# A layer norm's normalising pass and its bf16 copy, moved from VectorE to ScalarE

## The chip, the cores and the metric

The kernel runs on all eight NeuronCores of one Trainium2 chip, each with its own slice of the batch. Nothing is exchanged between the cores. The metric is the device time of the slowest core in microseconds.

## What is computed

Two "hybrid" layers, four stages in all, on x of shape (8, 2048, 1024) in f32. Each core has one batch element: 2048 tokens of 1024 features.

```python
x = x + attn_a(layernorm(x))   # stage 0: second layer norm inside with gamma, beta;
                               # qkv, causal softmax attention, 16 heads of 64
x = x + ffn(layernorm(x))      # stage 1
x = x + attn_b(layernorm(x))   # stage 2: no mask, projection with bias
x = x + ffn(layernorm(x))      # stage 3
# layernorm(x) = (x - mean) / sqrt(var + 1e-5)
# ffn: silu(bl(x, w_gate)) * bl(x, w_up), then bl(., w_down); inner size 4096
# bl: rows of x rounded to 8 bits by their own maximum, weights rounded to -1, 0, 1
```

## The kernel before

X stays in SBUF for the whole program as 16 token tiles of 128 partitions x 1024 f32. A list of operations is written in program order; each names what it reads and writes, and from that the program sets semaphore waits, also between two instructions of the same engine (TensorE excepted). Each engine then runs its own part of the list strictly in order. X counts as one resource, whichever tile is meant.

At first the three FFN weights are quantised and written to DRAM (until about 545 us). Then come the four stages. Each of them begins its work on a token tile with `ln_tile`:

1. VectorE sums the row (L390), ScalarE squares it with an accumulated sum (L393, into the scratch tile `stg`).
2. `stats`: five small VectorE instructions (L398 to L410), Ln and Exp on ScalarE (L413, L416) for 1/sqrt, and on VectorE mean times that (L419).
3. The normalising pass L425 from X into `xnf`, f32, 128x1024.
4. In mode "ln2" (stage 0) the sum (L429), the squares (L432) and `stats` once more, then L437 and the two passes for gamma and beta (L441, L444). In mode "quant" (stages 1 and 3) the row maximum (L448), three small ones, and ScalarE's scaling to int16 (L463) and copy to bf16 `stg` (L466). In the modes "ln2" and "plain" (stages 0 and 2) the bf16 copy is L469 on VectorE.
5. TensorE transposes `stg` in eight matmuls against the identity (L474) into PSUM, VectorE copies the result to `actT` (L482).

In the attention stages each tile's `ln_tile` is followed by `vunit`: 16 matmuls of the V product (L517) and its copy to `Vaug` on VectorE (L526). WV, the weights of it, are loaded once at the stage's beginning. `xnf` and `stg` are single buffers. Behind the 16 tiles come the projections to Q and K (L555), pass A for the row maxima (L590 to L647) and pass B with the exponentials on ScalarE (L676, L686, L701).

The FFN stages work in eight batches of two tiles: `ln_tile` for both, the gate and up products (L863, L875) with Silu on ScalarE (L885) and the product on VectorE (L892), and behind them the down projection of the batch before (L958 to L981), which ends with X += ... (L995). So the next batch's `ln_tile` reads an X that has just been written. The gate and up weights are fetched in two halves from the POOL queue, the down weights `Wdsl` in double-buffered strips from the SP queue.

Of the kernel before, what the change touches and what calls it, by code (L numbers as in the profile page):

```python
# [19 lines left out]
AF = mybir.ActivationFunctionType  # L20
ALU = mybir.AluOpType
AXX = mybir.AxisListType.X

B, T, D, H = 8, 2048, 1024, 16
# [87 lines left out]
def build_nc():  # L112
# [41 lines left out]
    def sb(name, shape, dtype, at=None):  # L154
        o = cur[0] if at is None else at
        t = nc.alloc_sbuf_tensor_at(name, shape, dtype, offset=o)
        offs[name] = o
        nbytes = int(np.prod(shape[1:])) * mybir.dt.size(dtype)
        cur[0] = o + (nbytes + 31) // 32 * 32
        return t  # L160

    X = sb("X", [128, NTT * D], F32)
# [4 lines left out]
    xnf = sb("xnf", [128, D], F32)  # L167
    stg = sb("stg", [128, D], BF16)
    stat = sb("stat", [128, 48], F32)
# [53 lines left out]
    E = S.emit  # L223
# [50 lines left out]
    def quant_matrix(midx, w_src, rows, cols, tag, dstT):  # L274
# [110 lines left out]
        reads=("swscr",), writes=("invsw_bc",))  # L385
    S.barrier()

    def ln_tile(mode, tt):
            xt = X[:, tt * D:(tt + 1) * D]
            E("dve", lambda e, x=xt: e.tensor_reduce(stat[:, 0:1], x, AXX,  # L390
                                                     ALU.add),
              reads=("X",), writes=("st0",))
            E("act", lambda e, x=xt: e.activation(stg[:, :], x, AF.Square,  # L393
                                                  accum_out=stat[:, 1:2]),
              reads=("X",), writes=("st1", "stg"))

            def stats(c_sum, c_sq, c_r, c_mr):
                E("dve", lambda e, cs=c_sum: e.tensor_scalar(  # L398
                    stat[:, 24:25], stat[:, cs:cs + 1], 1.0 / D, None,
                    ALU.mult), reads=("st%d" % c_sum,), writes=("stm",))  # L400
                E("dve", lambda e: e.tensor_tensor(
                    stat[:, 25:26], stat[:, 24:25], stat[:, 24:25], ALU.mult),
                  reads=("stm",), writes=("stm2",))
                E("dve", lambda e, cq=c_sq: e.tensor_scalar(
                    stat[:, 26:27], stat[:, cq:cq + 1], 1.0 / D, None,
                    ALU.mult), reads=("st%d" % c_sq,), writes=("stq",))
                E("dve", lambda e: e.tensor_tensor(
                    stat[:, 26:27], stat[:, 26:27], stat[:, 25:26],
                    ALU.subtract), reads=("stm2", "stq"), writes=("stq",))
                E("dve", lambda e: e.tensor_scalar(  # L410
                    stat[:, 26:27], stat[:, 26:27], LN_EPS, None, ALU.add),
                  reads=("stq",), writes=("stq",))
                E("act", lambda e: e.activation(stat[:, 27:28], stat[:, 26:27],  # L413
                                                AF.Ln),
                  reads=("stq",), writes=("stln",))
                E("act", lambda e, cr=c_r: e.activation(  # L416
                    stat[:, cr:cr + 1], stat[:, 27:28], AF.Exp, scale=-0.5),
                  reads=("stln",), writes=("st%d" % c_r,))
                E("dve", lambda e, cr=c_r, cm=c_mr: e.tensor_tensor(  # L419
                    stat[:, cm:cm + 1], stat[:, 24:25], stat[:, cr:cr + 1],  # L420
                    ALU.mult), reads=("stm", "st%d" % c_r),
                  writes=("st%d" % c_mr,))

            stats(0, 1, 2, 3)
            E("dve", lambda e, x=xt: e.tensor_scalar(  # L425
                xnf[:, :], x, stat[:, 2:3], stat[:, 3:4], ALU.mult,
                ALU.subtract), reads=("X", "st2", "st3"), writes=("xnf",))
            if mode == "ln2":
                E("dve", lambda e: e.tensor_reduce(stat[:, 4:5], xnf[:, :],  # L429
                                                   AXX, ALU.add),  # L430
                  reads=("xnf",), writes=("st4",))
                E("act", lambda e: e.activation(stg[:, :], xnf[:, :],  # L432
                                                AF.Square,
                                                accum_out=stat[:, 5:6]),
                  reads=("xnf",), writes=("st5", "stg"))
                stats(4, 5, 6, 7)
                E("dve", lambda e: e.tensor_scalar(  # L437
                    xnf[:, :], xnf[:, :], stat[:, 6:7], stat[:, 7:8], ALU.mult,
                    ALU.subtract), reads=("xnf", "st6", "st7"),
                  writes=("xnf",))  # L440
                E("dve", lambda e: e.tensor_tensor(  # L441
                    xnf[:, :], xnf[:, :], gamma_bc[:, :], ALU.mult),
                  reads=("xnf", "gamma_bc"), writes=("xnf",))
                E("dve", lambda e: e.tensor_tensor(  # L444
                    xnf[:, :], xnf[:, :], beta_bc[:, :], ALU.add),
                  reads=("xnf", "beta_bc"), writes=("xnf",))
            if mode == "quant":
                E("dve", lambda e: e.tensor_reduce(  # L448
                    stat[:, 8:9], xnf[:, :], AXX, ALU.max,
                    apply_absolute_value=True), reads=("xnf",),  # L450
                  writes=("st8",))
                E("dve", lambda e: e.tensor_scalar(
                    stat[:, 8:9], stat[:, 8:9], 1e-5, None, ALU.max),
                  reads=("st8",), writes=("st8",))
                E("dve", lambda e: e.reciprocal(stat[:, 9:10], stat[:, 8:9]),
                  reads=("st8",), writes=("st9",))
                E("dve", lambda e: e.tensor_scalar(
                    stat[:, 9:10], stat[:, 9:10], 127.0, None, ALU.mult),
                  reads=("st9",), writes=("st9",))
                E("dve", lambda e, tt=tt: e.tensor_scalar(  # L460
                    stat[:, 32 + tt:33 + tt], stat[:, 8:9], 1.0 / 127.0, None,
                    ALU.mult), reads=("st8",), writes=("rsx%d" % tt,))
                E("act", lambda e: e.activation(  # L463
                    qsc[:, :], xnf[:, :], AF.Copy, scale=stat[:, 9:10]),
                  reads=("xnf", "st9"), writes=("qsc",))
                E("act", lambda e: e.activation(stg[:, :], qsc[:, :], AF.Copy),  # L466
                  reads=("qsc",), writes=("stg",))
            else:
                E("dve", lambda e: e.tensor_copy(stg[:, :], xnf[:, :]),  # L469
                  reads=("xnf",), writes=("stg",))  # L470
            par = tt % 2
            pk = ("A0", "A1") if par == 0 else ("A2", "A3")
            for ic in range(NIC):
                E("pe", lambda e, ic=ic, p=par: e.matmul(  # L474
                    PA[:, p * 1024 + ic * 128:p * 1024 + (ic + 1) * 128],
                    stg[:, ic * 128:(ic + 1) * 128], ident[:, :],
                    start=True, stop=True),
                  reads=("stg", "ident"), writes=pk,
                  inc="pe" if ic == NIC - 1 else None)
            dstv = actT[:, :].rearrange("p (c t) -> p c t", c=NIC)[  # L480
                :, :, tt * 128:(tt + 1) * 128]
            E("dve", lambda e, p=par, dv=dstv: e.tensor_copy(  # L482
                dv, PA[:, p * 1024:(p + 1) * 1024].rearrange(
                    "p (c t) -> p c t", c=NIC)),
              reads=pk, writes=("actT%d" % tt,))

    def ln_stage(mode, hook=None):
        for tt in range(NTT):
            ln_tile(mode, tt)
            if hook is not None:  # L490
                hook(tt)
# [335 lines left out]
    def ffn():  # L827
# [174 lines left out]
        for bat in range(NTT // 2):  # L1002
            ln_tile("quant", 2 * bat)
            ln_tile("quant", 2 * bat + 1)
            gateup(bat, tail_quant_units(bat - 1) if bat > 0 else ())
            if bat > 0:
                tail_down(bat - 1)
# [107 lines left out]
```

How the kernel before makes its waits and increments, by code:

```python
        def replay(engine, eng):  # L1068
            for (e, fn, waits, inc, n) in S.ops:
                if e != engine:
                    continue
                best = {}
                for (sname, v) in waits:
                    if v > best.get(sname, -1):
                        best[sname] = v
                for sname, v in sorted(best.items()):
                    if v > 0 and last_wait.get((engine, sname), -1) < v:
                        eng.wait_ge(sems[sname], v)
                        last_wait[(engine, sname)] = v
                if fn is None:
                    continue
                inst = fn(eng)
                if inc is not None:
                    inst.then_inc(sems[inc], n)
```

## Time and profile before

| | before |
|---|---|
| median of three runs | 8256.87 us (8251.48, 8256.87, 8267.48) |
| profiled execution | 8252.33 us, span of its slowest core 8250.8 us |
| spans of the eight cores | 8218.4 to 8250.8 us |
| busy share of TensorE / VectorE / ScalarE | 61% / 35% / 20% |
| mean granted clock of TensorE | 0.65 |

The span runs from the first to the last instruction of the slowest core; the profiled execution's time is 1.5 us longer, for what lies around it. Shares are averages over stages with different limits. The kernel has no engine near full, so the question at each place is which engine's work the others wait for.

### The profile page before, as it was taken

How to read it: one execution, taken by the hardware profiler on the slowest of the kernel's cores; microseconds unless marked ns; L12 is line 12 of the kernel's file. 1: busy time of each engine (PE TensorE's matmuls, PEld its weight loads, DVE VectorE, ACT ScalarE, POOL GpSimd, SP SyncE). 2: the span in 40 equal slices, each digit the busy share in tenths (PEclk: the TensorE clock that was granted, in tenths of full speed). 3: DMA queues.
4: the chain of work that ended last, by engine and by line, in shares of the span. 5: the costliest groups of instructions: out<-in, count | busy, mean ns of one | idle time of the engine just before them, and what ended most of it. 6: DMA issues, size and time to landing. Idle time of an engine off the chain costs nothing.

```text
span 8250.8 us, 61625 instructions; the slowest of 8 cores (8218.4 to 8250.8 us)
## 1 busy us (share of the span) xinstructions
PE 4997.0 (61%) x15758; PEld 1588.6 (19%) x15942; DVE 2920.6 (35%) x5756; ACT 1677.2 (20%) x2784; POOL 423.2 (5%) x637
## 2 busy tenths in 40 slices
PE   0223266666666576666645777787777757666675
PEld 0111011111111222222211111111111123222221
DVE  2445233333333333323334244324333434323331
ACT  0321022222222211111001322332333221111110
POOL 0100000000000101000000000000000001000000
PEclk9856555555555688777776555555555568777876
DMA  8850300000000355444310000000000005444553
GB/s 226 287 185 0 45 1 3 3 3 3 3 3 1 105 153 171 138 142 131 119 32 6 2 2 3 3 1 3 3 3 1 1 13 173 145 144 133 153 154 120
DMA packets 260557, 580.78 MB, mean 70 GB/s; under 512 B 78396, under 2 KB 95548, under 8 KB 259772
## 3 DMA queue, kind: packets, MB, share of 16 engines
q0 software_dynamic: 101968, 400.97, 16.3%
q1 hardware_dynamic: 137388, 150.69, 6.8%
q10 hardware_dynamic: 20864, 25.17, 0.9%
q8 instruction: 145, 2.38, 0.1%
q14 instruction: 192, 1.57, 0.1%
HBM read 543.07 MB, written 48.50 MB: 72 GB/s over the span
## 4 chain that ended last, share of the span: by engine, by line
PE 40%; DVE 19%; DMA 18%; ACT 9%; issue 8%; another core or an unknown queue 2%; POOL 1%; DVEq 1%; ACTq 0%; SPq 0%; POOLq 0%; PEldq 0%
PE PB L701 9%; DMA Wdsl<-wd_tT 8%; PE PA L676 7%; ACT Etile L686 7%; DVE tiny L644 6%; DMA Wusl<-wu_tT 4%; PE PA L590 4%; PE PB L875 4%; PE PA L555 3%; PE PA L863 3%; PE PA L981 3%; PE PB L981 2%; PE PA L517 2%; DVE t2T L967 2%
## 5 line engine op out<-in xcount | busy, mean ns | idle before, releaser
L686 ACT ACTIVATE Etile<-PA 128x512 bf16<-128x512 f32 x1664 | 945.0, 596 | 2516.7 <-PE PA L676 2516.4
L701 PE MATMUL PB<-Etile,Vaug 128*65 128x512 bf16 x1664 | 1008.9, 614 | 506.1 <-POOL Etile L694 294.1
L676 PE MATMUL PA<-Qaug,Kaug 65*128 65x512 bf16 x1664 | 949.2, 626 | 164.4 <-DMA Qaug<-mrow_scr 164.4
L604 DVE TENSOR_REDUCE tiny<-PA 128x1 f32<-128x512 f32 (+2 forms) x832 | 531.6, 658 | 743.7 <-PE PA L590 681.2
L981 PE MATMUL PA<-Wdsl,t2T 128*128 128x512 bf16 x992 | 414.0, 507 | 395.8 <-DMA Wdsl<-wd_tT 365.9
L701 PEld LDWEIGHTS PB<-Etile,Vaug 128*65 128x65 bf16 x1664 | 223.2, 134 | 1522.7 <-issue 1522.3
L875 PE MATMUL PB<-Wusl,actT 128*128 128x512 bf16 x1990 | 481.5, 381 | 52.6 <-DMA Wusl<-wu_tT 49.0
L863 PE MATMUL PA<-Wgsl,actT 128*128 128x512 bf16 x2024 | 504.7, 392 | 3.8 <-issue 2.2
L590 PE MATMUL PA<-Kaug,Qaug 64*128 64x512 bf16 (+2 forms) x832 | 434.6, 577 | 101.9 <-DVE tiny L604 99.4
L474 PE MATMUL PA<-ident,stg 128*128 128x128 bf16 x512 | 64.8, 306 | 683.0 <-ACT stg L466 357.0
L981 PE MATMUL PB<-Wdsl,t2T 128*128 128x512 bf16 x1008 | 433.6, 522 | 2.4 <-issue 2.0
L995 DVE SCALAR_TENSOR_TENSOR X<-PA,tiny,X 128x1024 f32<-128x1024 f32 x16 | 20.5, 1284 | 1119.2 <-PE PA L981 1119.2
L739 DVE RECIPROCAL tiny<-PA 128x1 f32<-128x1 f32 x256 | 43.1, 168 | 1029.2 <-PE PA L734 1009.5
L393 ACT ACTIVATE stg<-X 128x1024 bf16<-128x1024 f32 x64 | 67.6, 1056 | 1590.4 <-DVE X L995 1070.5
L555 PE MATMUL PA<-actT,WQK 128*128 128x512 bf16 x994 | 295.8, 455 | 120.3 <-DMA WQK<-wa_qk 97.0
L892 DVE SCALAR_TENSOR_TENSOR tsb<-PB,tiny,gsl 128x512 f32<-128x512 f32 x256 | 191.9, 750 | 464.0 <-PE PB L875 426.5
L885 ACT ACTIVATE gsl<-PA,tiny 128x512 f32<-128x512 f32 x256 | 175.9, 687 | 708.4 <-PE PA L863 664.0
L875 PEld LDWEIGHTS PB<-Wusl,actT 128*128 128x128 bf16 x2048 | 197.0, 98 | 311.9 <-issue 91.9
L644 DVE TENSOR_REDUCE tiny<-PA 128x1 f32<-128x2048 f32 (+8 forms) x128 | 225.1, 1758 | 86.8 <-PE PA L626 69.8
L676 PEld LDWEIGHTS PA<-Qaug,Kaug 65*128 65x128 bf16 x1664 | 176.8, 128 | 407.4 <-issue 403.2
L863 PEld LDWEIGHTS PA<-Wgsl,actT 128*128 128x128 bf16 x2048 | 205.3, 101 | 255.8 <-issue 32.8
L626 PE MATMUL PA<-Kaug,Qaug 64*128 64x512 bf16 (+2 forms) x416 | 172.7, 548 | 113.8 <-DVE tiny L644 98.5
(126 smaller groups left out, 4494.0 us busy)
## 6 DMA issues: line engine op xcount, KB each, us to landing
Wdsl<-wd_tT SPq DMA_DIRECT2D x512, 256.0 KB, 2.7
Wgsl<-wg_tT POOLq DMA_DIRECT2D x128, 1024.0 KB, 7.2
Wusl<-wu_tT POOLq DMA_DIRECT2D x128, 1024.0 KB, 8.6
wch<-wg POOLq DMA_DIRECT2D x16, 2048.0 KB, 19.9
wch<-wu POOLq DMA_DIRECT2D x16, 2048.0 KB, 16.5
wch<-wd POOLq DMA_DIRECT2D x16, 2048.0 KB, 18.0
X<-x POOLq DMA_DIRECT2D x1, 8192.0 KB, 32.6
wg_tT<-wstg ACTq DMA_DIRECT2D x8, 1024.0 KB, 12.5
```

Source lines behind the costliest of these rows:

```text
L555: E("pe", lambda e, s=s, qn=qn, ic=ic: e.matmul(PA[:, (qn % 2) * 512:(qn % 2) * 512 + 512], WQK[:, ic * 256 + s * 128: ic * 256 + s * 128 ...
L590: Qh=Qh, Kh=Kh: e.matmul(PA[:, po:po + sn], Qh[0:64, qt * 128:(qt + 1) * 128], Kh[0:64, s0:s0 + sn], start=True, stop=True),
L604: E("dve", lambda e, sn=sn, po=po, tc=tc: e.tensor_reduce(tiny[:, tc:tc + 1], PA[:, po:po + sn], AXX, ALU.max), reads=(bank,), writes=("tm ...
L644: E("dve", lambda e, kend=kend, ps=ps: e.tensor_reduce(tiny[:, 0:1], ps[:, 0:kend], AXX, ALU.max), reads=bks, writes=("tmx0",))
L676: e.matmul(PA[:, po:po + 512], Kh[0:65, kt * 128:(kt + 1) * 128], Qh[0:65, qb * 512:(qb + 1) * 512], start=True, stop=True),
L686: E("act", lambda e, qb=qb, po=po: e.activation(Etile[:, qb * 512:(qb + 1) * 512], PA[:, po:po + 512], AF.Exp, scale=0.125), reads=("A%d" ...
L701: E("pe", lambda e, h=h, kt=kt, qb=qb, sk=sk: e.matmul(PB[0:65, qb * 512:(qb + 1) * 512], Vaug[:, kt * (H * 65) + h * 65: kt * (H * 65) + ...
L863: e.matmul(PA[:, q * 512:(q + 1) * 512], actT[:, ic * T + tt * 128: ic * T + (tt + 1) * 128], Wgsl[:, p * 4096 + ic * 512: p * 4096 + (ic ...
L875: e.matmul(PB[:, q * 512:(q + 1) * 512], actT[:, ic * T + tt * 128: ic * T + (tt + 1) * 128], Wusl[:, p * 4096 + ic * 512: p * 4096 + (ic ...
L885: E("act", lambda e, q=j: e.activation(gsl[:, :], PA[:, q * 512:(q + 1) * 512], AF.Silu, scale=tiny[:, q:q + 1]), reads=("A%d" % j, "scg%d ...
L892: e.scalar_tensor_tensor(tsb[:, q * INNER + c0:q * INNER + c0 + 512], PB[:, q * 512:(q + 1) * 512], tiny[:, 2 + q:3 + q], gsl[:, :], ALU.m ...
L981: E("pe", lambda e, q=j, i2=i2, n=n, p2=par2: e.matmul(PA[:, 1024 + n * 512:1024 + (n + 1) * 512] if q == 0 else PB[:, 1024 + n * 512:1024 ...
```

## The change

The pass L425 goes to ScalarE as an Identity activation with scale and bias read per partition. ScalarE adds its bias where VectorE subtracted the second scalar, so `stats` now forms minus the mean, and the second normalisation of mode "ln2" (L437, still on VectorE) adds too. The bf16 copy L469 of the modes "ln2" and "plain" goes to ScalarE as a Copy activation.

```diff
             def stats(c_sum, c_sq, c_r, c_mr):
                 E("dve", lambda e, cs=c_sum: e.tensor_scalar(
-                    stat[:, 24:25], stat[:, cs:cs + 1], 1.0 / D, None,
+                    stat[:, 24:25], stat[:, cs:cs + 1], -1.0 / D, None,
                     ALU.mult), reads=("st%d" % c_sum,), writes=("stm",))
...
             stats(0, 1, 2, 3)
-            E("dve", lambda e, x=xt: e.tensor_scalar(
-                xnf[:, :], x, stat[:, 2:3], stat[:, 3:4], ALU.mult,
-                ALU.subtract), reads=("X", "st2", "st3"), writes=("xnf",))
+            E("act", lambda e, x=xt: e.activation(
+                xnf[:, :], x, AF.Identity, scale=stat[:, 2:3],
+                bias=stat[:, 3:4]), reads=("X", "st2", "st3"),
+              writes=("xnf",))
...
                 E("dve", lambda e: e.tensor_scalar(
                     xnf[:, :], xnf[:, :], stat[:, 6:7], stat[:, 7:8], ALU.mult,
-                    ALU.subtract), reads=("xnf", "st6", "st7"),
+                    ALU.add), reads=("xnf", "st6", "st7"),
                   writes=("xnf",))
...
             else:
-                E("dve", lambda e: e.tensor_copy(stg[:, :], xnf[:, :]),
+                E("act", lambda e: e.activation(stg[:, :], xnf[:, :],
+                                                AF.Copy),
                   reads=("xnf",), writes=("stg",))
```

## Rows read from the trace of the kernel before

**Rows 1.** Head of the page and its busy line (us, share, instructions)
```profile
span 8250.8 us, 61625 instructions; the slowest of 8 cores (8218.4 to 8250.8 us)
PE 4997.0 (61%) x15758; PEld 1588.6 (19%) x15942; DVE 2920.6 (35%) x5756; ACT 1677.2 (20%) x2784; POOL 423.2 (5%) x637
```

**Rows 2.** Waits of TensorE, whole span: waiting, waited for, us, times, longest
```profile
PE PA L981 <- DMA Wdsl<-wd_tT: 365.9, 422, 2.1
PE PA L474 <- ACT stg L466: 357.0, 32, 12.9
PE PA L474 <- DVE stg L469: 326.1, 32, 20.6
```

**Rows 3.** Order of time in a tile of stage 0: start us, duration us, instruction, [idle before]
```profile
607.32 0.20 ACT L416 ACTIVATE stat<-stat 128x1 f32<-128x1 f32 x1
607.62 0.16 DVE L419 TENSOR_TENSOR stat<-stat 128x1 f32<-128x1 f32 x1 [0.69 <-ACT stat L416]
607.89 0.81 DVE L425 TENSOR_SCALAR xnf<-X,stat 128x1024 f32<-128x1024 f32 x1
608.80 1.06 ACT L432 ACTIVATE stg<-xnf 128x1024 bf16<-128x1024 f32 x1 [1.28 <-DVE xnf L425]
...
615.71 0.69 DVE L469 CAST stg<-xnf 128x1024 bf16<-128x1024 f32 x1
...
616.55 1.01 PE L474 MATMUL PA<-ident,stg 128*128 128x128 bf16 x8 [13.23 <-DVE stg L469]
```

**Rows 4.** Order of time in an FFN pair: ScalarE at its first tile, TensorE behind it
```profile
3047.75 1.15 ACT L463 ACTIVATE qsc<-xnf,stat 128x1024 int16<-128x1024 f32 x1 [3.39 <-DVE stat L460]
3048.99 1.06 ACT L466 ACTIVATE stg<-qsc 128x1024 bf16<-128x1024 int16 x1
...
3062.14 2.76 PE L863 MATMUL PA<-Wgsl,actT 128*128 128x512 bf16 x6
```

**Rows 5.** Groups by line (busy us, mean ns), L425 with min/median/max, and L413's loads
```profile
L463 ACT ACTIVATE qsc<-xnf,stat 128x1024 int16<-128x1024 f32 x32 | 36.7, 1147 | 110.6 <-DVE stat L460 110.6
L466 ACT ACTIVATE stg<-qsc 128x1024 bf16<-128x1024 int16 x32 | 33.8, 1056 | 2.9
L686 ACT ACTIVATE Etile<-PA 128x512 bf16<-128x512 f32 x1664 | 945.0, 596 | 2516.7 <-PE PA L676 2516.4
L885 ACT ACTIVATE gsl<-PA,tiny 128x512 f32<-128x512 f32 x256 | 175.9, 687 | 708.4 <-PE PA L863 664.0
L469 DVE CAST stg<-xnf 128x1024 bf16<-128x1024 f32 x32 | 22.2, 694 | 3.3
...
L425 DVE TENSOR_SCALAR xnf<-X,stat x64: 811/812/1189, 552.3 to 7973.7; 128x1024 f32<-128x1024 f32 x64
...
L413 ACT ACTIVATE stat<-stat x80: 202/203/203, 551.4 to 7972.8; 128x1 f32<-128x1 f32 x80
L413 ACT ACT_TABLE_LOAD  x15: 1283/1283/1283, 2871.5 to 7960.5; - x15
```

**Rows 6.** Order of time in a V product of stage 2: its weight loads
```profile
4211.96 0.15 PEld L517 LDWEIGHTS PA<-WV,actT 128*128 128x128 bf16 x1 [0.27 <-issue]
4212.37 0.96 PEld L517 LDWEIGHTS PA<-WV,actT 128*128 128x128 bf16 x5 [0.27 <-issue]
```

**Rows 7.** VectorE's copies of the V product and its wait before them; last their sum
```profile
582.82 1.23 DVE L526 CAST Vaug<-PA 128x1024 bf16<-128x1024 f32 x1 [19.48 <-PE PA L517]
625.66 1.23 DVE L526 CAST Vaug<-PA 128x1024 bf16<-128x1024 f32 x1 [6.77 <-PE PA L517]
...
4199.45 1.23 DVE L526 CAST Vaug<-PA 128x1024 bf16<-128x1024 f32 x1 [22.32 <-PE PA L517]
...
4341.02 1.23 DVE L526 CAST Vaug<-PA 128x1024 bf16<-128x1024 f32 x1 [5.14 <-PE PA L517]
4356.56 1.23 DVE L526 CAST Vaug<-PA 128x1024 bf16<-128x1024 f32 x1 [6.63 <-PE PA L517]
...
  PE PA L517: 213.4, 32
```

## The prediction

> **What bounds the kernel now.** I read the busy line of the page first, then the waits of TensorE, then the order of time inside one tile of each kind. No engine is full: TensorE works 61% of the span, VectorE 35%, ScalarE 20% [rows 1]. So a share says nothing; what matters is whether the two moved operations stand in a chain that something waits for. The waits of TensorE say that they do: its first transposes of each layer-norm tile wait 326.1 us for the bf16 copy `stg` of L469 (32 times, once per tile of the two attention stages) and 357.0 us for that of L466 (32 times, the two FFN stages) [rows 2]. All 64 tiles are there. The order of time shows why nothing fills these waits: in the attention stages the next tile's reduction on VectorE stands in the program behind the copies of the V product of this tile, and in the FFN stages the reduction reads X, which L995 has just written, after the down projection's last matmul.
>
> In a tile of stage 0 [rows 3] every step starts about 0.1 us after the step before it has ended: the product of L419 ends at 607.62 + 0.16 = 607.78 and L425 starts at 607.89; L425 ends at 608.70 and ScalarE's L432 starts at 608.80; the copy L469 ends at 616.40 and TensorE starts at 616.55. The reader is to see that there is no slack anywhere from L419 to L474: a nanosecond added to one of them moves TensorE by a nanosecond. In an FFN tile it is the same [rows 4].
>
> **The change, part by part.**
>
> *Handovers.* L425 moves between two VectorE instructions, so one handover inside VectorE on each side becomes one between engines. Rows for each kind: VectorE to VectorE 0.11 us (L419 to L425), VectorE to ScalarE 0.10 us (L425 to L432, as above), ScalarE to VectorE 0.10 us (L416 ends at 607.52, L419 starts at 607.62), ScalarE to ScalarE 0.09 us (L463 to L466, 3047.75 + 1.15 to 3048.99), all in [rows 3, 4]. The same-engine handovers wait on the semaphore too. So the handovers cost nothing more: 0, with 0.02 us per tile either way.
>
> *The normalisation (L425), 64 times.* On VectorE it takes 812 ns in the median tile [rows 5]. On ScalarE no Identity and no bias operand in memory stands in the trace. The nearest rows: a 128x1024 pass from f32 with nothing read per partition is 1056 ns (L466; L432, from f32, 1.06 us in [rows 3]); with a per-partition scale it is 1147 ns (L463), so that operand costs 91 ns. The 128x512 pair says the same: L885 with scale 687 ns, L686 without 596 ns, again 91 ns, and L885 writes f32, so the type of the output costs nothing [rows 5]. The new instruction reads two per-partition operands, scale and bias. Bounds: 1147 ns if the second is free, 1238 ns if it costs as much as the first. I take 1238, since the second is the same kind of fetch. Then 1238 - 812 = 426 ns a tile, times 64 = 27.3 us; with the lower bound 335 ns and 21.4 us.
>
> The Trainium skill, "ScalarE: Activation LUTs", section "What ACT_TABLE_LOAD costs", gives 186 ns plus 0.833 ns an element, and about 93 ns for each pointer operand, bias included: an estimate of 1225 ns for this instruction, and 26.4 us for the 64. Its 93 ns agrees with the 91 ns of the trace for the scale; that the bias costs as much is shown by no row here.
>
> *The bf16 copy (L469), 32 times, attention stages alone.* 694 ns on VectorE; on ScalarE 1056 ns, the time of L466, which is the same Copy from an int16 tile [rows 5]; L432, which reads f32, takes 1.06 too. 362 ns a tile, 11.6 us.
>
> *The sign.* L398 has the same shape with another constant, L437 adds instead of subtracting; both keep their 0.15 and 0.81 us. 0.
>
> *What VectorE gains.* 64 x 0.812 + 32 x 0.694 = 74 us of busy time leave it. They are worth nothing: its next instruction in the program (L448, L429 or L482) waits for the moved one or for the transposes behind it.
>
> *What stands behind it on ScalarE.* Behind the normalisation stand L432 or L463 (which read its result anyway), and in the attention stages the Square of the next tile, which waits for the transposes of this one and is read only behind this tile's V product. Nobody waits. ScalarE needs no second table for Copy and Square next to Ln and Exp: there are 15 table loads at L413 for its 80 instructions [rows 5], one for each turn from Silu back to Ln. I take Identity for another such function: 0.
>
> *What is hidden.* The first V product of stage 0 and of stage 2 waits for its weights WV: VectorE stands 19.48 and 22.32 us before these two [rows 7], 14 and 17 us longer than before the mean of the others (5.72, below). The first tile of both can be 0.79 us later for nothing: -1.6 us.
>
> Serial sum: 27.3 + 11.6 - 1.6 = 37.3 us.
>
> *TensorE's clock.* In the tile at 4208 us the weight loads of the V product come 0.41 us apart at first and then five in 0.96 us [rows 6]: half clock (1.2 GHz) after the pause, then the full 2.4 GHz. Where the rise falls differs from tile to tile, and VectorE's wait for the product shows it: in stage 2 it falls tile by tile to 5.14, jumps to 6.63, and falls again; 5.14 is the lowest, 6.77 the highest [rows 7]. The sum over all 32 is 213.4, without the two that wait for weights (19.48 and 22.32) 171.6 over 30, or 5.72 us. The order is so regular because the next pass starts a nearly fixed time behind the last; the passes sit more in the cheap end of the spread. A tile that is 0.79 us longer leaves this pattern. If the rise then falls anywhere in the spread, the mean is (5.14 + 6.77)/2 = 5.95: 0.23 x 30 = 7 us more. Bounds by the same rows: all at 5.14, -17 us; all at 6.77, +32 us. I take +7. In the FFN stages the first gate matmuls behind each pair of tiles have such a rise too, 16 of them, with no pattern to lose: 0, a few us either way.
>
> Sum: +44 us, or 0.54%. The profiled execution took 8252.33 us around a span of 8250.8; with the sum it is 8296. The median of the three runs shown is 8256.87, 4.5 us above it; on that base the forecast is 8301 us.
>
> The Trainium skill's "ScalarE: Activation LUTs", section "Rules for kernel authors", says that additions and multiplications belong on VectorE, which speaks against this change. The trace agrees for both: 812 ns against at least 1147, and 694 against 1056.
>
> **Rivals.**
>
> *A, the forecast:* all 64 tiles pay in full, with the clock's part anywhere in its bounds: 8257 + 37 - 17 to 8257 + 37 + 32, so 8277 to 8326.
>
> *B, the cover is larger than the waits show:* part of the longer tile meets waits that would be there anyway (weights in front of the FFN's first gate product, as at the first V product), or the clock's part goes to its cheap end with a free bias operand: 37.3 - 5.8 - 17 = +14 us, 8271 us, no change that could be told. Against it: behind the pair that ends at 3062 the gate matmuls start at 3062.14 [rows 4] with no wait for weights, because both halves were loaded during the down projection.
>
> *C, Identity is not in the table that holds Ln and Exp:* then each tile pays a load for it, and a load back at the next Ln (1283 ns each [rows 5]). 64 x 1.283 for the first, and 80 - 15 = 65 x 1.283 for the second: 82 + 83 = 165 us more, 8466 us. For it: only Copy and Square have been seen beside Ln and Exp. Against it: these two run on both sides of a turn from Silu to Ln with no load of their own, so simple functions seem to be in every table.
>
> *D, faster, by the waits of the down projection for its weights:* L981 waits 365.9 us for them in 422 pieces [rows 2], while all eight cores read. The same program takes from 8218.4 to 8250.8 us on the eight cores [rows 1]. If the longer pauses moved the cores apart so that their reads collide less, this wait could shrink. It decides from 44 + 17 = 61 us, a sixth of the wait; at a fifth (73 us) the time would be 8228. Against it: each pause grows by 0.85 us in an FFN batch, on all cores alike.
>
> **How the numbers follow.** A measurement of this kernel tells about 0.2%, 16.5 us, from no change: the runs shown span 8251.5 to 8267.5. Chances: A 0.83, B 0.09, C 0.04, D 0.04. So slower by over 0.2%: 0.87; within: 0.09; faster: 0.04. Range: A's bounds, widened at the low end to B (8272) and at the high end by 2 us to 8328; C and D are left out.
>
> **What would show it.** In the new profile: Identity at 1238 ns (1147 if the bias is free), Copy at 1056, both x64 and x32 and with ScalarE's busy time up by 79 + 34 = 113 us; VectorE's down by 74. TensorE's waits at L474: 326.1 up by 32 x 0.79 = 25 us, 357.0 up by 32 x 0.43 = 14 us. VectorE's waits at L526 without the first two at a mean of 5.95, and no longer in the falling order of [rows 7]. Table loads no more than before (15 at L413). The forecast is wrong if the waits at L474 grow by less (then something covers them), if a table load stands before Identity, or if the waits of L981 on its weights move by more than 20 us.

## The result, and the profile after

The changed kernel takes 8306.98 us in the median of ten runs against 8256.31 us before, a ratio of 1.0059 with a 95% interval of 1.0049 to 1.0069: 49 us slower, where +44 us (8301 us) was forecast. The profiled execution has a span of 8295.7 us on its slowest core, 44.9 us more than before; the eight cores lie between 8257.4 and 8295.7 us.

The busy line of the page after, to be held against that in [rows 1]:

```profile
span 8295.7 us, 61675 instructions; the slowest of 8 cores (8257.4 to 8295.7 us)
PE 5002.4 (60%) x15758; PEld 1588.7 (19%) x15942; DVE 2846.4 (34%) x5660; ACT 1790.9 (22%) x2880; POOL 424.5 (5%) x637
```

VectorE has lost 74 us of work and ScalarE has got 114 us. Neither is near full in either kernel, so the line alone would let one expect nothing. The waits of TensorE (waiting, waited for, us, times, longest), against [rows 2]:

```profile
PE PA L983 <- DMA Wdsl<-wd_tT: 371.9, 429, 1.9
PE PA L476 <- ACT stg L467: 370.7, 32, 13.6
PE PA L476 <- ACT stg L470: 349.5, 32, 21.0
```

The transposes of the 32 FFN tiles wait 13.7 us longer (370.7 against 357.0), those of the 32 attention tiles 23.4 us (349.5 against 326.1). The wait for the down weights has moved by 6 us only. The order of time inside a tile of stage 0 shows the two new instructions in the chain of [rows 3]:

```profile
608.62 0.16 DVE L419 TENSOR_TENSOR stat<-stat 128x1 f32<-128x1 f32 x1 [0.69 <-ACT stat L416]
608.87 1.24 ACT L425 ACTIVATE xnf<-X,stat 128x1024 f32<-128x1024 f32 x1 [0.36 <-DVE stat L419]
...
610.21 1.22 DVE L430 TENSOR_REDUCE stat<-xnf 128x1 f32<-128x1024 f32 x1 [1.44 <-ACT xnf L425]
...
615.79 1.23 DVE L445 TENSOR_TENSOR xnf<-xnf,beta_bc 128x1024 f32<-128x1024 f32 x1
617.11 1.06 ACT L470 ACTIVATE stg<-xnf 128x1024 bf16<-128x1024 f32 x1 [3.94 <-DVE xnf L445]
618.32 1.01 PE L476 MATMUL PA<-ident,stg 128*128 128x128 bf16 x8 [14.00 <-ACT stg L470]
```

The product ends at 608.78, Identity starts 0.09 us later; it ends at 610.11 and VectorE starts 0.10 us later. So the handover between engines costs what the one inside VectorE cost. VectorE now sits idle for 1.44 us while ScalarE does what VectorE had done in 0.81.

The groups of the two instructions and of the table loads (as in [rows 5]):

```profile
L425 ACT ACTIVATE xnf<-X,stat 128x1024 f32<-128x1024 f32 x64 | 79.3, 1239 | 22.9 <-DVE stat L419 22.9
L470 ACT ACTIVATE stg<-xnf 128x1024 bf16<-128x1024 f32 x32 | 33.8, 1056 | 64.5 <-DVE xnf L445 63.0
L413 ACT ACT_TABLE_LOAD x15 | 19.2, 1283 | 27.7 <-DVE stat L410 27.7
```

1239 ns and 1056 ns, and 15 table loads at L413 as before: Identity needs none. Last, VectorE's copies of the V product in stage 2, with its wait for the product in brackets (as [rows 7]), and under them the sum over all 32:

```profile
4232.77 1.23 DVE L528 CAST Vaug<-PA 128x1024 bf16<-128x1024 f32 x1 [6.77 <-PE PA L519]
4247.65 1.23 DVE L528 CAST Vaug<-PA 128x1024 bf16<-128x1024 f32 x1 [5.56 <-PE PA L519]
4263.62 1.23 DVE L528 CAST Vaug<-PA 128x1024 bf16<-128x1024 f32 x1 [6.64 <-PE PA L519]
4278.54 1.23 DVE L528 CAST Vaug<-PA 128x1024 bf16<-128x1024 f32 x1 [5.40 <-PE PA L519]
4294.42 1.23 DVE L528 CAST Vaug<-PA 128x1024 bf16<-128x1024 f32 x1 [6.56 <-PE PA L519]
...
  PE PA L519: 221.2, 32
```

The slow fall from 6.6 to 5.14 is gone; dear and cheap passes alternate. Without the two that wait for weights (19.50 and 20.67) the mean of 30 is 6.03 us on this core, against 5.72; in the mean of the eight cores it is 5.98 against 5.74. That this is TensorE's clock shows in the granted clock of the V part of stage 2: 0.70 before and 0.65 after, in the mean of the eight cores.

Where the time went, stage by stage. The stretches run from VectorE's first reduction of a stage to the memset of Kaug (the layer norm and V part), from there to the first reduction of the next stage (the attention's body), and over the FFN stages, the last of which is taken up to the start of its last X += ...; each number is the mean of the eight cores, in us:

| | V part, stage 0 | body 0 | FFN 1 | V part, stage 2 | body 2 | FFN 3 |
|---|---|---|---|---|---|---|
| before | 359.9 | 1875.7 | 1377.3 | 246.9 | 2428.6 | 1373.3 |
| after | 371.1 | 1880.3 | 1380.7 | 263.6 | 2439.4 | 1379.7 |
| difference | +11.2 | +4.6 | +3.4 | +16.7 | +10.8 | +6.4 |

The V parts grow by 27.9 us and the FFN stages by 9.8, together 37.7. That is near what the two operations should do, and somewhat less: the forecast's own terms come to 44. The bodies grow by 15.4 us, and no instruction in them has changed. The quantisation ahead of stage 0 was 11 us shorter in this execution; it scatters by that much from one profile to the next (the first reduction starts between 528 and 557 us).

### The profile page after: what moved, and what is told of

Read it like the earlier page. It is cut to its first block, busy times and chain, and to the rows that moved or that the text cites. A ratio compares the mean times of both kernels' runs of the same rounds, so it can differ in the third digit from the quotient of the medians.

```text
span 8295.7 us, 61675 instructions; the slowest of 8 cores (8257.4 to 8295.7 us)
## 1 busy us (share of the span) xinstructions
PE 5002.4 (60%) x15758; PEld 1588.7 (19%) x15942; DVE 2846.4 (34%) x5660; ACT 1790.9 (22%) x2880; POOL 424.5 (5%) x637
## 4 chain that ended last, share of the span: by engine, by line
PE 40%; DMA 18%; DVE 18%; ACT 11%; issue 8%; another core or an unknown queue 2%; POOL 1%; DVEq 1%; ACTq 0%; SPq 0%; POOLq 0%; PEldq 0%
PE PB L703 9%; DMA Wdsl<-wd_tT 8%; PE PA L678 7%; ACT Etile L688 7%; DVE tiny L646 6%; DMA Wusl<-wu_tT 4%; PE PA L592 4%; PE PB L877 4%; PE PA L557 4%; PE PA L865 3%; PE PA L983 3%; PE PA L519 2%; PE PB L983 2%; DVE t2T L969 2%
## 5 line engine op out<-in xcount | busy, mean ns | idle before, releaser
L983 PE MATMUL PA<-Wdsl,t2T 128*128 128x512 bf16 x992 | 406.3, 498 | 399.6 <-DMA Wdsl<-wd_tT 371.9
L476 PE MATMUL PA<-ident,stg 128*128 128x128 bf16 x512 | 64.7, 306 | 720.1 <-ACT stg L467 370.7
L393 ACT ACTIVATE stg<-X 128x1024 bf16<-128x1024 f32 x64 | 67.6, 1056 | 1487.3 <-DVE X L997 1070.7
L557 PE MATMUL PA<-actT,WQK 128*128 128x512 bf16 x994 | 305.4, 467 | 115.7 <-DMA WQK<-wa_qk 92.4
## 6 DMA issues: line engine op xcount, KB each, us to landing
wg_tT<-wstg ACTq DMA_DIRECT2D x8, 1024.0 KB, 12.6
```

The lines of the kernel that those rows point to most:

```text
L557: E("pe", lambda e, s=s, qn=qn, ic=ic: e.matmul(PA[:, (qn % 2) * 512:(qn % 2) * 512 + 512], WQK[:, ic * 256 + s * 128: ic * 256 + s * 128 ...
L983: E("pe", lambda e, q=j, i2=i2, n=n, p2=par2: e.matmul(PA[:, 1024 + n * 512:1024 + (n + 1) * 512] if q == 0 else PB[:, 1024 + n * 512:1024 ...
```

## The experiments

**One half at a time.** First the normalisation alone, the copy left on VectorE (called e1 below; the difference is against the changed kernel):

```diff
-                E("act", lambda e: e.activation(stg[:, :], xnf[:, :],
-                                                AF.Copy),
+                E("dve", lambda e: e.tensor_copy(stg[:, :], xnf[:, :]),
                   reads=("xnf",), writes=("stg",))
```

> Only the normalising pass L425 goes to ScalarE (with its sign); the bf16 copy of the attention stages stays on VectorE. Theory (serial chain plus TensorE's clock): 64 x (1.239 - 0.812) = 27.3 us, less 0.9 us hidden in the two first tiles, plus 3 to 8 us for the V passes that leave their cheap pattern: +30 to +35 us, ratio 1.0036 to 1.0042. TensorE's waits at its layer-norm transposes 14 us longer in the attention stages and 14 us in the FFN stages. Rival (the FFN stages hide their part, as the spans of single stages may suggest: they grew by 3 and 6 us where 7 each were due): +16 us, ratio 1.002.

Measured: ratio 1.0038 (1.0024 to 1.0051), +31 us. The transposes wait 368.8 us in the FFN stages (357.0 before) and 338.3 in the attention stages (326.1), on its slowest core. Each stage pays, with +7.8 and +9.7 us in the V parts and +2.0 and +9.6 in the FFN stages, whose cores differ by 30 us. The first expectation holds, though the two waits grew by 12 us each where 14 were expected; the rival's 1.002 lies below the interval.

Then the copy alone, in the kernel before (e2):

```diff
-                E("dve", lambda e: e.tensor_copy(stg[:, :], xnf[:, :]),
+                E("act", lambda e: e.activation(stg[:, :], xnf[:, :],
+                                                AF.Copy),
                   reads=("xnf",), writes=("stg",))
```

> Only the bf16 copy L469 of the attention stages goes to ScalarE. Theory: 32 x (1.056 - 0.694) = 11.6 us, less 0.7 us hidden, plus 3 to 8 us of clock: +14 to +19 us, ratio 1.0017 to 1.0023; the FFN stages keep their time. Rival (what costs is instructions on ScalarE with two operands in memory, not the length of the chain): the copy has none, so no change that can be told.

Measured: 1.0024 (1.0014 to 1.0035), +20 us, with +5.8 and +8.7 us in the V parts and -3.5 and +1.0 in the FFN stages, where nothing was moved. It is a little above the 14 to 19 us expected, which lie inside the interval. The two halves make 31 + 20 = 51 us, the change 49, each half with an interval of about 10 us to either side. The rival is out: an instruction without operands in memory costs too.

**The same length with no work moved.** If only the length of the chain counts, redundant work on VectorE must cost the same (e3, against the kernel before):

```diff
                 xnf[:, :], x, stat[:, 2:3], stat[:, 3:4], ALU.mult,
                 ALU.subtract), reads=("X", "st2", "st3"), writes=("xnf",))
+            E("dve", lambda e: e.tensor_scalar(
+                xnf[:, 0:253], xnf[:, 0:253], 1.0, None, ALU.mult),
+              reads=("xnf",), writes=("xnf",))
...
             else:
+                E("dve", lambda e: e.tensor_scalar(
+                    xnf[:, 0:153], xnf[:, 0:153], 1.0, None, ALU.mult),
+                  reads=("xnf",), writes=("xnf",))
                 E("dve", lambda e: e.tensor_copy(stg[:, :], xnf[:, :]),
```

> The kernel before with both operations still on VectorE, and one redundant VectorE pass more in each place, a multiplication by 1 of the first 253 columns of xnf behind L425 (some 0.32 us and 0.11 us of handover) and of 153 columns before L469 (some 0.25 us and 0.11 us): the chain gets as long as the change makes it, with no work moved. Theory (only the length of the chain counts): the same time as the changed kernel, +45 to +50 us, V passes waited for 6.0 us in the mean. Rival (the handover between engines or ScalarE's queue costs something of its own): less than the changed kernel by over 10 us.

Measured: 1.0054 (1.0040 to 1.0068), +45 us. Its V parts are 371.7 and 263.9 us against 371.1 and 263.6 of the changed kernel. Its transposes wait 349.1 and 369.1 us, against 349.5 and 370.7, and the V passes are waited for 5.95 us in the mean of 30. So in these parts it doesn't matter which engine works or that two are involved; the chain's length is all. Only its bodies differ: 1878.7 and 2432.2 us.

**A longer tile at another length.** Four redundant passes ahead of L469 (e4, against the kernel before):

```diff
             else:
+                E("dve", lambda e: e.tensor_scalar(
+                    xnf[:, 0:1024], xnf[:, 0:1024], 1.0, None, ALU.mult),
+                  reads=("xnf",), writes=("xnf",))
...
+                E("dve", lambda e: e.tensor_scalar(
+                    xnf[:, 0:375], xnf[:, 0:375], 1.0, None, ALU.mult),
+                  reads=("xnf",), writes=("xnf",))
                 E("dve", lambda e: e.tensor_copy(stg[:, :], xnf[:, :]),
```

> The kernel before with four redundant VectorE passes in front of L469, in the attention stages alone: three multiplications by 1 of xnf in full (0.81 us and 0.10 us of handover each) and one of 375 columns (0.40 us): each of the 32 tiles gets 3.2 us longer. If the length of the tile, through the place in the V pass at which TensorE's clock rises, moves the wait for the pass, this length should bring the waits back to the cheap end, 5.2 to 5.4 us in the mean of 30 (5.72 before, 6.03 with the change): 32 x 3.24 - 6.5 - 12 = +85 us, ratio 1.0103. Rival (any longer tile leaves the cheap pattern, the waits go to 6.0): +106 us, ratio 1.0128.

Measured: 1.0093 (1.0080 to 1.0107), +77 us. Part of the expectation was mis-sized, as the order of time in one tile of stage 2 shows:

```profile
4243.87 0.69 DVE L469 TENSOR_SCALAR xnf<-xnf 128x1024 f32<-128x1024 f32 x1
...
4246.27 0.36 DVE L478 TENSOR_SCALAR xnf<-xnf 128x375 f32<-128x375 f32 x1
4246.73 0.69 DVE L481 CAST stg<-xnf 128x1024 bf16<-128x1024 f32 x1
4248.69 1.22 DVE L494 CAST actT<-PA 128x1024 bf16<-128x1024 f32 x1 [1.27 <-PE PA L486]
4255.32 1.23 DVE L538 CAST Vaug<-PA 128x1024 bf16<-128x1024 f32 x1 [5.41 <-PE PA L529]
```

With a constant factor a full pass takes 0.69 us, not the 0.81 of L425 with its two operands per partition; the four come to 4246.73 - 4243.87 = 2.86 us a tile. For 32 tiles that is 91.5 us, less 2 x 2.86 in the two first tiles, 86 us; with waits of 6.03 us in the other 30 it would be +95, and with this kernel's it is +81. The waits are 202.7 us in all on this core, 17.34 and 18.56 of them for weights, so 5.56 us in the mean of 30 (5.59 in the mean of the eight cores): lower than before (5.72), though the tile is longer, and not as low as the 5.2 to 5.4 expected for a tile of 3.2 us more. What follows: a longer tile doesn't by itself cost more at the V pass. The wait goes with the length at hand, and the change's 0.79 us is a dear one.

**Is it the second operand?** The changed kernel with the constant 0 as bias, which leaves out the subtraction of the mean (e9):

```diff
                 xnf[:, :], x, AF.Identity, scale=stat[:, 2:3],
-                bias=stat[:, 3:4]), reads=("X", "st2", "st3"),
+                bias=0.0), reads=("X", "st2", "st3"),
```

> The changed kernel with the constant 0 as bias of the Identity, so the mean is not subtracted in the first normalisation; the rest of the work stays. Theory (each operand read per partition costs the same 91 ns): 1147 ns instead of 1239 in each of 64 instructions, 6 us less in all. Rival (the 1239 ns are Identity's own): 1239 ns still.

```profile
L425 ACT ACTIVATE xnf<-X,stat x64: 1147/1147/1148, 545.5 to 8001.1; 128x1024 f32<-128x1024 f32 x64
```

1147 ns (shortest/median/longest) against 1239: the bias costs 92 ns, as much as the scale. Its one run took 8279.85 us, 8 us under the changed kernel's one further run (8288.08, below); a single run each can't settle a difference of 6.

**The bodies, again.** Both kernels once more, unchanged:

> The changed kernel as it is, one more look. In its first profile the attention body of stage 2 (from the Kaug memset behind the last tile to the first reduction of stage 3), which the change doesn't touch, took 2439 us in the mean of the eight cores, 2429 in the kernel before. Theory (the place of the clock's rises there differs from execution to execution): within 2429 to 2436 this time. Rival (the change sets them, through where the stage begins): 2439 again, all cores above 2435.

> The kernel before as it is, one more look on the same chip. The same stretch: theory, anywhere from 2427 to 2436 in the mean; rival, 2429 again. The V passes wait 5.7 us in the mean of 30 as in the first profile, since their order is set by the tile's length and not by the execution.

Measured, means of the eight cores: the changed kernel 1884.0 us in the body of stage 0 and 2437.5 in that of stage 2 (single cores 2433.8 to 2439.9); the kernel before 1876.1 and 2428.9. In the first profiles it was 1880.3 and 2439.4 against 1875.7 and 2428.6. So my expectation that this was the luck of one execution has fallen. The difference comes back, some 6 us in the body of stage 0 and 10 in that of stage 2, though not quite as the rival said, since single cores lie below 2435. The kernel with the constant bias, which also has both operations on ScalarE, shows it a third time: 1880.2 and 2436.9. The V passes of the second execution of the kernel before wait 217.1 us in all on core 0, against 213.4, so 5.80 us in the mean of 30. In stage 2 of core 0 they come in the same order as in the first profile, pass by pass within 0.05 us; in its stage 0, and in stage 2 of five other cores, single passes differ by over 1 us. What comes back for a tile of this length is the mean (5.63 us in stage 2 both times, over all cores) and not each single wait.

The traces also show where most of this time lies: in the projections to Q and K (L555, in the changed kernel L557), 512 matmuls in each body. These two rows, for core 1 in the body of stage 2, before and after, give the window, its length and the busy time of these matmuls, and of their weight loads:

```profile
4395.20:6821.70 2426.50, 151.25 (x512) 54.11 (x512) 0.56 0.02 3
4428.10:6867.80 2439.70, 159.86 (x512) 55.75 (x512) 0.55 0.02 3
```

In the mean of the eight cores TensorE is busy with them for 147.8 us in the body of stage 0 and 151.5 in that of stage 2 before, 151.5 and 158.8 after; in the second pair 148.8 and 150.4 against 154.9 and 156.7. That is 11 us of the 15.4, and 12.4 of the 16.5. Pauses aside, two of these matmuls in a row start either some 0.22 us apart (granted clock 1.0) or 0.43 us (0.5). In the body of stage 2 the slow steps go from 144 to 175 a core, in that of stage 0 from 127 to 142. So it is the clock once more, in bursts that come eight times in each body, and not an instruction of its own. Why it rises later in them after the change, no run shows.

**Taking the chain apart.** If everything is one chain through three engines, then overlapping its parts must give far more than any choice of engine. In the attention stages VectorE's copy of a V product goes behind the next tile's layer norm (e5_vcopy_later, engines as before the change):

```diff
-    def ln_stage(mode, hook=None):
+    def ln_stage(mode, vmm, vcopy):
         for tt in range(NTT):
-            ln_tile(mode, tt)
-            if hook is not None:
-                hook(tt)
+            ln_pre(mode, tt)
+            if tt > 0:
+                vcopy(tt - 1)
+            ln_post(tt)
+            vmm(tt)
+        vcopy(NTT - 1)
```

`ln_pre` is `ln_tile` up to `stg`, `ln_post` its transposes and the copy to `actT`; `vmm` holds the 16 matmuls of `vunit` and `vcopy` its copy to `Vaug`.

> The kernel before with one order changed, in the attention stages alone: VectorE's copy of a tile's V product is issued behind the next tile's layer norm up to stg, just ahead of the transposes, so that VectorE works on the next tile while TensorE multiplies. Theory (the stage is one chain through VectorE, ScalarE and TensorE): the wait for the V product, 5.7 us in each of 30 tiles, overlaps the next tile's 6 to 13 us of layer norm, and the 1.1 us of the copy too, under the transposes: 30 x 5 to 6.8, 150 to 200 us less, ratio 0.976 to 0.982. Rival (TensorE's half clock or the PSUM banks keep the order of before): under 50 us.

Measured: 0.9746 (0.9730 to 0.9762), 8045.63 us, 210 us less, somewhat more than the 150 to 200 expected. The V parts take 247.7 and 143.9 us (359.9 and 246.9). The order of time in a tile of stage 2 shows why:

```profile
4181.59 3.61 PE L526 MATMUL PA<-WV,actT 128*128 128x512 bf16 x16 [2.16 <-DVE actT L484]
...
4184.69 0.81 DVE L425 TENSOR_SCALAR xnf<-X,stat 128x1024 f32<-128x1024 f32 x1
4185.60 0.69 DVE L469 CAST stg<-xnf 128x1024 bf16<-128x1024 f32 x1
4186.21 1.22 DVE L539 CAST Vaug<-PA 128x1024 bf16<-128x1024 f32 x1
4186.44 0.61 PE L476 MATMUL PA<-ident,stg 128*128 128x128 bf16 x8 [1.24 <-DVE stg L469]
4187.34 1.22 DVE L484 CAST actT<-PA 128x1024 bf16<-128x1024 f32 x1
```

The V product of 3.61 us runs beside the next tile's layer norm, and the copy L539 beside the transposes, with no wait ahead of it. The eight transposes take 0.61 us instead of 1.01, and the product, for which VectorE had waited 5.7 us, is done in 3.61: the granted clock from its first to its last matmul is 1.00, the 2.4 GHz level. Not every tile is like this one. Of the 15 products behind the first in stage 2, ten take 3.61 us or less on this core and five 4.96 to 5.30, with half the clock at their beginning; the mean of the eight cores is 4.10 us there (5.37 in the kernel before), and in stage 0, where the layer norm of a tile takes longer, it is 5.61 as before. How much of the gain in stage 2 is the clock's, no run separates. The same with the change in it (e6):

> The same order with the change in it (both operations on ScalarE). Theory: the layer norm is still the chain, so the move costs against e5_vcopy_later what it costs against the kernel before, 32 x 0.79 in the attention stages and 32 x 0.43 in the FFN stages, +39 us, without the clock's part. Rival (now that the V product overlaps, the tile is bound by TensorE in stage 2, and the move is free there): +26 us or less.

Measured: 0.9779 (0.9765 to 0.9794), 8074.51 us, some 27 us above the one before by the ratios. The V parts grow by 10.1 and 11.4 us, the FFN stages by 4.9 and 7.6. So stage 2 pays nearly in full (16 x 0.79 = 12.6), and the move is not free there. But that doesn't show that TensorE bounds no tile: in some 5 of the 15 tiles behind the first of stage 2 in e5_vcopy_later, and some 6 in this kernel, the transposes start right behind the V product before them, with no wait for `stg`; and the mean V product behind the first has grown from 4.10 to 4.84 us, at a lower clock. How much of the 11.4 us is the layer norm's and how much the clock's stays open. The total doesn't decide: the intervals of the two ratios leave 18 us on either side of 27, which holds both the rival's +26 and my +39; the V parts and FFN stages of the eight cores sum to +34.

Then the FFN stages, where the layer norms of the next pair go into the down projection of the batch before (e7_ln_in_down):

```diff
             for i2 in range(32):
                 par2 = i2 % 2
+                if nxt and i2 == 0:
+                    ln_pre("quant", nxt[0])
+                if nxt and i2 == 14:
+                    ln_post(nxt[0], 0)
+                    ln_pre("quant", nxt[1])
+                if nxt and i2 == 28:
+                    ln_post(nxt[1], 0)
...
-            ln_tile("quant", 2 * bat)
-            ln_tile("quant", 2 * bat + 1)
+            if bat < 2:
+                ln_tile("quant", 2 * bat)
+                ln_tile("quant", 2 * bat + 1)
...
-                tail_down(bat - 1)
+                tail_down(bat - 1, (2 * bat + 2, 2 * bat + 3)
+                          if bat + 1 < NTT // 2 else ())
```

> e5_vcopy_later and in the FFN stages, for the batches 2 to 7, the layer norm of the next pair issued inside the down projection of the batch before (its reductions and passes ahead of the strips 0 and 14, its transposes ahead of the strips 14 and 28), while TensorE waits for weights there anyway. Engines as before the change. Theory: 12 of the 16 pairs vanish from the chain, 22 us each: 265 us less than e5_vcopy_later, minus a few us for the 16 transposes in each down projection. Rival (the down projection is bound by its weights and by the queue of VectorE, and the transposes stop it at the two places): under 150 us less.

Measured: 0.9412 (0.9396 to 0.9428), 7775.32 us, 270 us under e5_vcopy_later. Its waits of TensorE:

```profile
PE PA L1001 <- DMA Wdsl<-wd_tT: 421.3, 413, 3.2
...
PE PA L476 <- DVE stg L469: 130.9, 26, 20.2
...
PE PA L476 <- ACT stg L466: 85.9, 8, 12.2
```

Only 8 of the 32 FFN tiles are waited for, 85.9 us against 357.0; the down projection waits 52 us more for its weights than in e5_vcopy_later (369.2). The FFN stages take 1220.6 and 1229.6 us (1374.9 and 1369.5). With the change in it (e8):

> The same with the change in it. Theory (the move costs only where its chain is not covered): against e7_ln_in_down the 12 covered pairs cost nothing, so only the attention stages (25 us) and four open pairs (3.4 us) pay: +28 us, against +39 of e6 over e5. Rival (the move costs in the FFN stages whatever covers it): +39 us.

Measured: 0.9454 (0.9440 to 0.9468), 7808.75 us, 35 us above e7_ln_in_down by the ratios, with 18 us of uncertainty. The slowest core decides that, and in these two kernels the FFN stages of single cores lie anywhere from 1197 to 1262 us. The means of the eight cores tell more: the V parts pay 10.6 and 12.7 us, the FFN stages +4.8 and -4.2, zero in sum, where e6 paid 12.5 over e5. That speaks for the expectation (where the chain is covered the move is free), but the scatter is larger than the effect, so I call it supported and not settled.

## Why the prediction was right

*Which chain counts.* All 64 tiles were said to stand in the chain. The waits at the transposes grew by 23.4 and 13.7 us where 25 and 14 were forecast; the halves moved alone (e1, e2) show that each piece pays, and the redundant work (e3) that mere length costs the same.

*The prices.* 1238 and 1056 ns were taken, 1239 and 1056 measured. The open one was the bias operand; the upper bound was right, and e9 shows it by taking it away. The Trainium skill's "ScalarE: Activation LUTs", section "What ACT_TABLE_LOAD costs", which gives the bias operand the same 93 ns as the scale, agrees with the 92 and 91 ns; its 1225 ns is 14 ns short of the 1239.

*Handovers at 0.* Held: 0.09 and 0.10 us, and e3, which has no new handover between engines, has the same V parts.

*What is hidden, -1.6 us.* Core 0 alone can't tell it: VectorE's two long waits went from 19.48 and 22.32 to 19.50 and 20.67, and they differ by 2 to 5 us from core to core. In the mean of the eight cores they went from 22.0 and 22.8 to 20.7 and 21.7 us, 2.3 us less in all, and by 2.5 us in the second pair of profiles. So the term held, with a size that is rough.

*TensorE's clock, +7 us.* The waits for the V product came to 6.03 us on core 0 against the 5.95 taken, +9.4 us over 30; in the mean of the eight cores it is +7.1 us, and +6 in the second pair. One reading was off: the longest of the 30 waits of core 0 is 6.81 us and not 6.77, which would have made the term 8 us. The reason given, that a tile of another length leaves the order it had, held too, but the step from there to "anywhere in the spread" was a guess, and that its number came out is luck: the new order is just as regular (6.5 and 5.4 in turn), and e4 shows a longer tile with cheaper passes. The sign depended on the length.

*What the sum left out.* The bodies of the attention stages were costed at nothing. They take 15.4 us more (16.5 in the second pair of profiles). So the closeness of 44 to 49 is partly luck: the V parts and the FFN stages give 38 where the sum had 44, the bodies 15, and the rest is scatter, most of it ahead of stage 0. Some 11 of the 15 us lie in the projections to Q and K, which run longer at half clock. The prediction had looked for such a part of the clock in the V passes and in the FFN's gate matmuls, and not in these bursts. Why the clock rises later in them stays open. It isn't the luck of an execution, since it came back. It isn't the length of the V part alone, since e3 has the same and its bodies took 3.0 and 3.6 us more than before. e1 and e2, with half of the change each, have bodies of 1873.5 and 1874.2, 2432.1 and 2432.0 us.

*Rivals.* The smaller cost by hidden tiles (B), the extra table loads (C) and shorter weight waits (D: 371.9 against 365.9) did not come.

## What to carry to other kernels

Ask of a moved operation whether its old engine was late for anybody, and not how busy it was: in a serial chain each operation belongs on the engine that does it soonest, and the load of the engines is nothing to balance. If both engines wait for each other most of the time, the order in the program is the thing to change: here one such change gave 2.5% and two gave 5.9%, where the choice of engine is worth 0.6%. Price an activation by its length and by its operands read per partition, 91 to 92 ns each here.

## What the runs showed of the hardware that was not expected

A VectorE pass over 128x1024 f32 in SBUF takes 812 ns with two operands per partition and 0.69 us with a constant. In a stage that repeats tile by tile, the wait for the same 16 matmuls came in an order that repeated too: falling from 6.6 to 5.14 us before, alternating between about 5.4 and 6.5 us after 0.79 us more per tile, and at 5.4 to 5.6 us, with one of 5.9, after 2.86 us more. With the pauses partly filled, two thirds of the products of stage 2 took 3.6 us. Stretches that the change doesn't touch took 5 to 11 us more, most of it in matmuls that ran longer at half clock, and did so again in another execution of the same program.
